# Three streams for two in a transformer of two layers: first attention, experts with cross attention, and last layer of three successive sequences

## The reference

```python
# block 0: self attention (causal) and cross attention to ctx, 16 heads of 8, one projection
y = softmax(mask(q @ k.T / sqrt(8))) @ v + softmax(qc @ kc.T / sqrt(8)) @ vc
x = x + y @ Wp + bp                                 # x normed before q, k, v, qc
# block 0: all 8 experts (128 -> 512 -> 128), weighted by a softmax over the top 2 logits
x = x + sum_e w[:, e] * (relu(xn @ W1[e] + b1[e]) @ W2[e] + b2[e])
# block 1: one-head attention to ctx (256 x 256 scores)
x = x + softmax(q1 @ k1.T) @ v1
# block 1: 16 heads of 64; values mixed per token and head from the top 2 of 8 expert values,
# outputs gathered per token over the top 2 of 8 output experts
v[h] = sum_e mix[t, h, e] * (xn @ Wv[e]);  at[h] = softmax(q[h] @ k[h].T / 8) @ v[h]
x = x + sum_h sum_e mask_o[t, h, e] * (at[h] @ Wo[e])
```

## Time and profile before

| | us |
|---|---|
| median of 3 runs | 1716.87 (1716.63 to 1721.53) |
| profiled execution, its own time | 1711.72 |
| its span, first to last instruction | 1710.0 |
| TensorE busy | 1310.1 |
| VectorE busy | 718.0 |
| ScalarE busy | 488.1 |
| mean granted clock of TensorE | 0.718 |

### The profile page before, as it was taken

The page is one execution under the profiler, slowest core; times in us unless marked ns, Lnnn a source line. Parts: engine busy times, 40 slices in busy tenths (PEclk is TensorE's granted clock), DMA queues, the critical chain, the costliest instruction groups (busy, mean ns, idle before and its releaser), DMA issues.

```text
span 1710.0 us, 21323 instructions
## 1 busy us (share of the span) xinstructions
PE 1310.1 (77%) x8530; PEld 1008.1 (59%) x8530; DVE 718.0 (42%) x1958; ACT 488.1 (29%) x1003; POOL 77.1 (5%) x134
## 2 busy tenths in 40 slices
PE   2777668887679777896788777897688876897566
PEld 2446545775458654685457654596457754586366
DVE  2623492335822385225813376214832349122700
ACT  0233314224133232333143232333132231332120
POOL 0010001000010000100010000100010000100000
PEclk9657766787667875697658875697666976677655
DMA  5000010311012110301103110301103101121131
GB/s 157 7 1 4 0 31 4 64 44 26 12 28 43 38 28 10 64 19 28 34 1 64 44 29 10 58 13 41 25 10 64 44 16 22 26 41 38 37 59 46
DMA packets 197498, 56.85 MB, mean 33 GB/s; under 512 B 173029, under 2 KB 193303, under 8 KB 197399
## 3 DMA queue, kind: packets, MB, share of 16 engines
q1 hardware_dynamic: 195318, 51.30, 14.2%
q10 hardware_dynamic: 2080, 4.19, 0.8%
HBM read 31.36 MB, written 24.12 MB: 32 GB/s over the span
## 4 chain that ended last, share of the span: by engine, by line
PE 60%; DVE 23%; ACT 7%; issue 4%; DMA 3%; SPq 0%; ACTq 0%; DVEq 0%
PE bank L942 8%; PE bank L766 8%; PE bank L792 7%; DVE negmax L1179 6%; PE bank L692 6%; PE bank L904 4%; PE bank L618 4%; ACT pa L1012 3%; DVE negc L1331 3%; PE bank L925 3%; PE bank L707 2%; DVE qk_lo L1323 2%; DMA at<-at_d 2%; PE bank L956 2%; PE bank L717 2%
## 5 line engine op out<-in xcount | busy, mean ns | idle before, releaser
L1012 ACT ACTIVATE pa<-bank 128x512 f32<-128x512 f32 x224 | 123.4, 597 | 351.5 <-PE bank L707 266.2
L942 PE MATMUL bank<-vb,pb 128*128 128x65 f32 x1024 | 147.2, 315 | 12.2 <-issue 12.2
L942 PEld LDWEIGHTS bank<-vb,pb 128*128 128x128 f32 x1024 | 145.8, 232 | 16.4 <-issue 16.3
L766 PE MATMUL bank<-xnT_a,w 128*128 128x256 f32 x512 | 145.9, 436 | 0.0
L1179 DVE TENSOR_REDUCE negmax<-bank 128x2 f32<-128x512 f32 (+1 forms) x224 | 138.8, 682 | 16.2 <-PE bank L653 11.6
L1029 ACT ACTIVATE pa<-bank,b_c 128x256 f32<-128x256 f32 x256 | 107.3, 470 | 127.8 <-PE bank L766 126.4
L792 PEld LDWEIGHTS bank<-w,pa 128*128 128x128 f32 x1024 | 124.1, 193 | 3.0
L792 PE MATMUL bank<-w,pa 128*128 128x128 f32 x1024 | 124.1, 276 | 0.0
L766 PEld LDWEIGHTS bank<-xnT_a,w 128*128 128x128 f32 x512 | 106.7, 219 | 21.9 <-issue 7.0
L1087 ACT ACTIVATE pb<-bank 128x512 f32<-128x512 f32 x128 | 69.5, 595 | 169.7 <-PE bank L908 169.4
L692 PE MATMUL bank<-pa,va 128*32 128x256 f32 (+1 forms) x1024 | 101.8, 550 | 16.4 <-ACT pa L1012 15.9
(11 more groups left out here) (231 smaller groups left out, 1972.3 us busy)
## 6 DMA issues: line engine op xcount, KB each, us to landing
v_d<-vb SPq DMA_DIRECT2D x16, 512.0 KB, 5.1
vb<-v_d SPq DMA_DIRECT2D x16, 512.0 KB, 5.7
at_d<-at SPq DMA_DIRECT2D x32, 256.0 KB, 2.1
at<-at_d SPq DMA_DIRECT2D x32, 256.0 KB, 4.3
pv_d<-pvs SPq DMA_DIRECT2D x8, 512.0 KB, 2.8
pvs<-pv_d SPq DMA_DIRECT2D x16, 256.0 KB, 4.3
w<-in_L_ffn_W_dram ACTq DMA_DIRECT2D x1, 2048.0 KB, 10.4
bd<-mix_d SPq DMA_DIRECT2D x128, 8.0 KB
```

The lines of the kernel that those rows point to most:

```text
L766: mm = pe.matmul(BA[u % 2][:, c * T:(c + 1) * T], w1[:, e, f:f + P], xnT_a[:, :], start=True, stop=True)
L942: mm = pe.matmul(BB[2 + qt][:, i * (DH + 1):(i + 1) * (DH + 1)], pb[:, h % NPB, kt * T + qt * P:kt * T + (qt + 1) * P], vb[:, kt, h, :], s ...
L1012: nc.scalar.activation(pa[:, e % NPA, :], BA[e % 2][:, :], ACT.Exp, scale=SC0).then_inc(S["a_ex"], 1)
```

## The change

The two streams become three. A keeps the first attention and the next sequence's input norm; X takes a_norm2, the router, the experts (step a_expert is divided in a_hid, one hidden half, and a_yout, one expert's output) and the cross attention; B stays. X starts 1.03 and B 2.06 periods after A, so that three successive sequences are at work. HOLD is a new table. The banks are dealt out anew: three for A, two for X, three for B. a_max goes in groups of three tiles, b_split and b_max over three banks; the values of the first attention, the mixed values and the two halves of b_attend have one bank each where they had two, X's hidden tiles one, X's outputs one. So steps gain waits for the copy out of a bank that they had not: values(n) waits for output n-1, the second half of b_mix and of b_attend for the first, the fourth turning in a_shift and a_heads for the first tile's use.

x_f has two halves by the sequence's parity, and takes the place of x_a up to the first expert's accumulation; cxT_a has two; the input norm gets its own xn and xnT_f; the experts' hidden tiles and the cross attention's operands move from pa to a new hx of three tiles; pa has 8 tiles, pb 6. f_load stands before a_heads, and its load of x_f waits for the first accumulation of two sequences back. The number of matmuls, activations and VectorE instructions is as before.

```diff
-        BA, BB = banks[:4], banks[4:]
+        BA, BX, BB = banks[:3], banks[3:5], banks[5:]
...
-        x_f = sb("x_f", [P, NT, C])
+        x_f = sb("x_f", [P, 2, NT, C])
         cx_f = sb("cx_f", [P, NT, CC])
         x_a = sb("x_a", [P, NT, C])
         xnT_a = sb("xnT_a", [P, T])
-        cxT_a = sb("cxT_a", [CC, T])
+        cxT_a = sb("cxT_a", [CC, 2, T])
+        xnT_f = sb("xnT_f", [P, T])
...
-        NPA = 9
+        NPA = 8
...
-        hT = pa[:, 0:4, :].rearrange("p u (c n) -> p u c n", c=2)
+        hx = sb("hx", [P, 3, 512])
+        hT = hx[:, :, :].rearrange("p u (c n) -> p u c n", c=2)
...
-        NPB = 8
+        NPB = 6
...
-        ln["f"]["xn"] = ln["a"]["xn"]
-        y = ln["a"]["xn"]
-        xn_a, xn_b = ln["a"]["xn"], ln["b"]["xn"]
+                      xn=sb(f"xn_{s}", [P, NT, C])) for s in "abf"}
+        y = ln["f"]["xn"]
+        xn_a, xn_b, xn_f = ln["a"]["xn"], ln["b"]["xn"], ln["f"]["xn"]
...
-        NBLK = NS // 4
+        NBLK = (NS + 2) // 3
...
-        OUT_AT = {4: 0, 5: 1, 7: 2, 8: 3, 11: 4, 12: 5}
+        OUT_AT = {4: (0, 1), 7: (2,), 8: (3,), 11: (4, 5)}
...
-        RUNS = {"a_max": 2, "a_score": 7, "a_expert": 4, "b_score": 2}
-        LAG = 0.04
         HOLD = {
-            "a_stack": 1.0, "a_values": 1.29, "a_max": (3.44, 7.52, 2.92, 10.2), "a_shift": 3,
-            "a_score": (1.92, 2.01), "a_lastpv": 2.07, "a_heads": 4.0, "a_project": 1.88, "a_norm2": 4.26,
-            "a_norm2_apply": 1.04, "a_router": 6.19, "a_expert": (4, 4.01), "a_b2": 12, "c_norm": 3.31,
-            "f_norm": 0.77, "f_load": 0, "c_norm_apply": 1.29, "c_qkv": 3.77, "f_norm_apply": 1, "c_max": 1.57, "c_turn": 1.62,
-            "c_out": 1.74, "b_norm": 2.87, "b_norm_apply": 3, "b_gates": 2.98, "b_split": 0.98, "b_top2": 3,
-            "b_max": 1.4, "b_shift": 7.07, "b_score": (4, 4, 4, 4), "b_mix": 4.5,
-            "b_attend": 4, "b_weigh": 5, "b_gather": 5, "b_out": 6}
-
-        def share(step):
-            name, i = step
-            return HOLD[name][i // RUNS[name]] if name in RUNS else HOLD[name]
-
+            "a_stack": 2, "a_values": 3, "a_max": 3, "a_shift": 5, "a_score": 4, "a_lastpv": 4, "f_load": 0, "a_heads": 5,
+            "a_project": 5, "f_norm": 8, "f_norm_apply": 3,
+            "a_norm2": 8, "a_norm2_apply": 2, "a_router": 4, "a_hid": 3, "a_yout": 6, "a_b2": 4, "c_norm": 8,
+            "c_norm_apply": 2, "c_qkv": 5, "c_max": 4, "c_turn": 4, "c_out": 4,
+            "b_norm": 9, "b_norm_apply": 2, "b_gates": 5, "b_split": 2, "b_top2": 0, "b_max": 2.2, "b_shift": 4,
+            "b_score": 4, "b_mix": 5, "b_attend": 6, "b_weigh": 7, "b_gather": 3, "b_out": 5}
 
         STEPS_A = [("a_stack", u) for u in range(8)] + [("a_values", 0)]
         STEPS_A += [("a_max", m) for m in range(NBLK)] + [("a_shift", 0)]
-        STEPS_A += [("a_score", n) for n in range(2 * PER_J)] + [("a_lastpv", 0), ("a_heads", 0), ("a_project", 0)]
-        STEPS_A += [("f_load", 0), ("a_norm2", 0), ("a_norm2_apply", 0), ("a_router", 0)]
-        STEPS_A += [("a_expert", e) for e in range(E)] + [("a_b2", 0)]
-        STEPS_A += [("c_norm", 0), ("f_norm", 0), ("c_norm_apply", 0), ("c_qkv", 0), ("f_norm_apply", 0),
-                    ("c_max", 0), ("c_turn", 0), ("c_out", 0)]
+        STEPS_A += [("a_score", n) for n in range(2 * PER_J)] + [("a_lastpv", 0), ("f_load", 0), ("a_heads", 0), ("a_project", 0)]
+        STEPS_A += [("f_norm", 0), ("f_norm_apply", 0)]
+        STEPS_X = [("a_norm2", 0), ("a_norm2_apply", 0), ("a_hid", 0), ("a_router", 0), ("a_hid", 1)]
+        for e in range(E):
+            STEPS_X += [("a_hid", 2 * e + 2)] if e + 1 < E else []
+            STEPS_X += [("a_yout", e)]
+            STEPS_X += [("a_hid", 2 * e + 3)] if e + 1 < E else []
+        STEPS_X += [("a_b2", 0), ("c_norm", 0), ("c_norm_apply", 0), ("c_qkv", 0), ("c_max", 0), ("c_turn", 0), ("c_out", 0)]
         STEPS_B = [("b_norm", 0), ("b_norm_apply", 0), ("b_gates", 0)]
         STEPS_B += [("b_split", u) for u in range(4)] + [("b_top2", 0)] + [("b_split", u) for u in range(4, 8)] + [("b_top2", 1)]
         STEPS_B += [("b_max", 0), ("b_max", 1), ("b_top2", 2)] + [("b_max", m) for m in range(2, 8)] + [("b_shift", 0)]
-        STEPS_B += [("b_score", 0), ("b_score", 1), ("b_mix", 0), ("b_mix", 1)] + [("b_score", p) for p in range(2, 4)]
-        for hg in range(1, 4):
-            STEPS_B += [("b_attend", hg - 1), ("b_score", 2 * hg + 2), ("b_score", 2 * hg + 3)] if hg < 3 else [("b_attend", 2)]
-        STEPS_B += [("b_attend", 3), ("b_weigh", 0), ("b_gather", 0), ("b_gather", 1), ("b_out", 0)]
-
-        def merged(lag):
+        STEPS_B += [("b_score", 0), ("b_score", 1), ("b_mix", 0), ("b_mix", 1), ("b_score", 2), ("b_attend", 0)]
+        STEPS_B += [("b_score", 3), ("b_score", 4), ("b_attend", 1), ("b_score", 5), ("b_score", 6), ("b_attend", 2)]
+        STEPS_B += [("b_score", 7), ("b_attend", 3), ("b_weigh", 0), ("b_gather", 0), ("b_gather", 1), ("b_out", 0)]
+
+        def merged():
 
             timed = []
...
-            for steps, offset in ((STEPS_A, 0.0), (STEPS_B, 1.0 + lag)):
-                total, at_ = sum(share(step) for step in steps), 0
+            for steps, offset in ((STEPS_A, 0.0), (STEPS_X, 1.03), (STEPS_B, 2.06)):
+                total, at_ = sum(HOLD[name] for name, _ in steps), 0
...
-                        if q > 0:
-                            sp.wait_ge(S["a_x1"], upto("a_x1", 0))
-                        sp.dma_start(x_f[:, :, :], x_tiles[:, q * NT:(q + 1) * NT, :]).then_inc(S["f_in"], 16)
+                        if q > 1:
+                            sp.wait_ge(S["a_acc"], upto("a_acc", 1 - 2 * E))
+                        sp.dma_start(x_f[:, q % 2, :, :], x_tiles[:, q * NT:(q + 1) * NT, :]).then_inc(S["f_in"], 16)
...
-                        sc, qt, _, gp = MAXS[4 * m]
+                        tiles = range(3 * m, min(3 * m + 3, NS))
...
+                        for c in range(4):
+                            for n in tiles:
+                                sc, qt, j, gp = MAXS[n]
+                                rows = slice(32 * j, 32 * j + 32)
                                 if m > 0 and c == 0:
...
-                        bank, pair, i = BA[2 + n % 2], j // 2, j % 2
+                        bank, pair, i = BA[2], j // 2, j % 2
                         pe.wait_ge(S["a_ex"], upto("a_ex", 2 * PER_J * pair + (8 if sc == CROSS else 2 * PER_J)))
                         if sc == SELF:
                             pe.wait_ge(S["a_sl"], upto("a_sl", 6 * pair + 6))
-                        if n >= 2:
-                            pe.wait_ge(S["a_ot"], upto("a_ot", n - 1))
+                        if n >= 1:
+                            pe.wait_ge(S["a_ot"], upto("a_ot", n))
...
-                    def hidden(u):
+                    def a_hid(u):
                         e, fp = u // 2, u % 2
-                        if u >= 2:
-                            pe.wait_ge(S["a_ha"], upto("a_ha", u - 1))
+                        if u == 0:
+                            pe.wait_ge(S["a_xc"], upto("a_xc", 1))
+                            pe.wait_ge(s_experts, 32)
+                        else:
+                            pe.wait_ge(S["a_ha"], upto("a_ha", u))
                         for c in range(2):
                             f = (2 * fp + c) * P
-                            mm = pe.matmul(BA[u % 2][:, c * T:(c + 1) * T], w1[:, e, f:f + P], xnT_a[:, :],
+                            mm = pe.matmul(BX[0][:, c * T:(c + 1) * T], w1[:, e, f:f + P], xnT_a[:, :],
                                            start=True, stop=True)
                         mm.then_inc(S["a_h"], 1)
...
+                    def a_yout(e):
                         pe.wait_ge(S["a_ha"], upto("a_ha", 2 * e + 2))
-                        if e == 1:
+                        if e == 0:
                             pe.wait_ge(S["a_lgc"], upto("a_lgc", 1))
-                        if e >= 2:
-                            pe.wait_ge(S["a_acc"], upto("a_acc", e - 1))
+                        else:
+                            pe.wait_ge(S["a_acc"], upto("a_acc", e))
                         for t in range(NT):
                             for f in range(FC):
-                                mm = pe.matmul(BA[2 + e % 2][:, t * P:(t + 1) * P],
-                                               hT[:, (2 * e + f // 2) % 4, f % 2, t * P:(t + 1) * P], w2[:, e, f, :],
+                                mm = pe.matmul(BX[1][:, t * P:(t + 1) * P],
+                                               hT[:, (2 * e + f // 2) % 3, f % 2, t * P:(t + 1) * P], w2[:, e, f, :],
...
-                        else:
-                            pe.wait_ge(S["b_ve"], upto("b_ve", NT))
-                        for i in range(T8):
-                            g = T8 * half + i
-                            for t in range(NT):
-                                rows = slice(64 * t, 64 * t + 64)
```

(17 more changed lines are left out.)

278 lines of the change are left out of this document (128 added, 150 removed).

## The result

The changed kernel takes 1835.72 us (median of 4 runs, 1833.88 to 1841.98); the kernel before took 1719.06 beside it. The ratio is 1.0685, 95% interval 1.0652 to 1.0718: slower by 117 us, where 1685 us had been forecast in a range up to 1790.

The account below looks back on a forecast made before the run. TensorE was taken to set most of the time, VectorE one stretch of each period. Period 75 + 83 + 9 + 9.7 + 5 + 3.5 = 185 us; 572 + 6 x 185 = 1682, given as 1685 us; range 1555 to 1790.

Parts of the forecast that it names:

- The ends: Set-up and the stretches at the run's start and end without three full streams: 572 us in all, give or take 15.
- DVE's stretch: Part of each period set by VectorE (row maxima, splits, top-2): 63.5 us of work, taken as 75 us at 85% busy.
- PE's work: TensorE's matmuls in the period's other stretches: 100 us at today's clocks, 17 saved by a higher clock, 83 remain.
- Waits inside PE's steps: New single-bank waits in values, b_mix, b_attend and a_heads that no other stream can fill: 9.7 us a period.
- 5 for b_attend 0: Wait before b_attend's first step for the mixed values' round trip, partly covered by other steps: 5 us a period.
- b_mix's lost side-by-side run: b_mix's two halves run one after the other instead of alternating: 3.5 us a period, bounds 0 to 5.
- X's single banks at nothing: Stream X's one-bank chain, 33 us, runs under A and B within eight tenths of a period, so costed at nothing.
- Rival 2: Single-bank pauses in TensorE's steps keep its clock low; period 200 us, time 1772 us; chance 0.30.
- Its sign: Rival 2's mark in the new profile: successive sequences' marks 190 us or more apart, clock at 0.72 or under.
- Rival 3: Experts' 48 us at clock 1.00 run at 0.50 between narrow matmuls; period about 221, time 1900 us; chance 0.06.
- theory T: Expectation from the follow-up experiments, not the prediction: the third stream itself spreads the dense work, whatever the banks.

Follow-up runs that it names:

- the filler: Two-stream kernel with b_attend on one bank (1788.34 us), plus two fp32 matmuls with unread results put in place of the wait: 1764.50 us.
- 1696: Three-stream kernel with b_attend in half-steps on one bank and b_mix's two halves side by side on two banks: 1695.86 us.
- 1704: Kernel 1696 with the values as steps of their own and the mixed values (vb) loaded back ahead of bd: 1704.22 us.
- 1707: Three-stream kernel with two banks for b_attend and b_mix, values as own steps, vb loaded earlier, b_attend in half-steps, no pause step: 1706.78 us.
- two banks alone: Three-stream kernel with b_attend's second half on a second bank borrowed from the scores, other one-bank forms kept: 1786.30 us.
- the pause alone: Three-stream kernel with an empty step of 8 shares (about 11 us) in stream B's plan before b_attend 0: 1795.11 us.

## Why the prediction was wrong

By its own steps:

- *The ends*, 572 us: measured 580. The first attention alone ends at 145.2 for 147, the first x_mid stands at 274 for 272, the last layer alone within 3 us; the 8 us are in X of the last sequence beside B (160 for 152). Right within the 15 that were given.
- *DVE's stretch*, 75 us: measured 82. DVE's work in it was sized right (62.6 for 63.5 us), its density was not, 76% for the assumed 85%. 7 us of the error a period. And the stretch was taken as given by the order's shares; shifting B shows it was a choice of the offset, worth 39, 52 and 61 us in three kernels.
- *PE's work*, "64.2 us at 0.62 to 0.85, 17 us saved, 83 remain": this is the step that failed. Measured, in place of 83 + 3.5, are 109.2 us; 23 of the 24 us by which the period was missed (DVE's 7 more are nearly offset by 6 less of waiting). The work at full clock was about right (77 us for 87 - 11.4). But the granted clock over PE's stretches went from 0.76 to 0.70, where 17 us had been booked for a rise. The bounds of the term were too narrow in kind: "nothing saved" kept the experts' stretch at 1.00, as if only the narrow stretches had a clock to gain or lose. What took its place: where b_attend stood in the dense stretch at 1.00, its single bank and the wait for the round trip now put pauses, and b_attend and its neighbours run at the lower level. That such pauses do it is shown in two streams and argued in three (one bank for b_attend in two streams: 41 us of longer matmuls beside 31 of waiting; the filler took 24 us off by adding work; the cut into half-steps took 100 us of busy time off with no idle time saved).
- *Waits inside PE's steps*, 9.7 us a period, and 5 for b_attend 0: idle time in PE's stretches was 17.8 in all for 23.7. One by one: between b_attend's halves 0.73 for 1.0; before b_attend 0 4.0 in this period and 5.1 in the mean of the six, for 5; b_mix 11.5/8 = 1.4 for 1.8; the values (23.6 - 16.4)/8 = 0.9 for 2.55, the one that was well off (there are three waits for the copy a sequence, as forecast, but of 0.65 us, and the waits for the exponentials fell from 15.9 to 7.1 us in all). As idle time they were priced well, and as a cause of a lower clock at nothing.
- *b_mix's lost side-by-side run*, 3.5 us: the same change in two streams cost 34/8 = 4.3, and L925 5.6 a sequence; the changed kernel's line has (81.6 - 48.8)/8 = 4.1 more. Near the upper bound of 5.
- *X's single banks at nothing*: 21.9 us before L765, 2.7 a sequence, not nothing; but the same form costs the two-stream kernel 60 us of idle time and 107 in all, so that most of it was covered, as argued.

Rival 2, "the period does not shrink", had the mechanism: pauses of about 1 us from single banks keep the clock down. Its sign, marks 190 or more apart at a clock of 0.72 or under, is what came (209 and 0.717). It was given 0.30 and a period of 200 us; its price was short too, since it let the clock only stay at 0.62 in the outer stretches, and the level fell inside, so that the time lies above the whole range. The argument held against it, that 9.7 us of new pauses are less than what a third stream covers, compared microseconds of idle time, where the place of a pause counted. Rival 3, that the experts lose their clock, came true in part: their two groups took 65 us more.

The Trainium skill, "TensorE: Matmul & The Clock Gate", section "A second HAM failure mode: psum-queue depth-cycling", says that brief idle between groups of matmuls, from cycling through PSUM banks, makes the clock go down and up again. The kernel with one bank for b_attend and the one with its pauses filled (1788 and 1764 us, share 0.42 and 0.65) agree in this: filling the pause returned the level. Here the idle time comes from one bank used twice in a row, and not from going through several. The rule would have made rival 2 the likeliest, and the direction bears it out; it gives no price.

What stays open: why b_attend's share in half-steps falls from 0.64 (1696) to 0.47 (1704 and 1707) once the values are steps of their own and vb is loaded earlier, though idle time falls; it isn't the second bank. Open too is why shortening the waits before b_attend by 41 us left the time unchanged, and how the single bank and the long wait share the low level of b_attend in the changed kernel: two banks alone brought the share from 0.27 to 0.38, the pause alone to 0.55, and two banks with the values' steps and a wait of 9.5 us left it at 0.26. Drawing the experts together into b_attend's stretch would test theory T by itself. One such order was written, but in it the engines wait for one another in a circle, so it has no time, and T by itself stays untested. Shown is only that the third stream is no obstacle to a clock of 0.77; without the shift of B it brings a period of 190 us for 197.

## What to carry to other kernels

Before a stream is added, write down for each PE step that loses a bank which engine it then waits for in its middle, and cut the step there, so that the other streams' steps fill the wait; a wait inside a dense stretch is to be priced at its length and again at the slower matmuls around it (31 and 41 us here). Put the stretches that another engine bounds (here the row maxima of two streams) at different places of the period: one offset was worth 2 to 3% here. And look at busy time, not at the mean clock or the idle time alone: the mean was 0.717 and 0.718 in two kernels 117 us apart.

## What the runs showed of the hardware

- Adding 128 matmuls (49.6 us of them) in pauses of 0.7 to 0.8 us made a kernel 24 us faster: the pauses' 24 us went, and all other matmuls together ran 51 us shorter (b_attend's share at the high level 0.65 for 0.42).
- One and the same step stands at either level in one execution: in the two-stream kernel b_attend 0 takes 3.76 us for 32 matmuls at 720 us, and at 1110 us 20 of them take 4.50. An edit elsewhere (one bank for the values) moved b_attend's busy time from 147 to 130 us. Judged by these 17 us, an estimate: some 15 us of difference between two such kernels can come from this alone.
- Matmuls on rows 0 to 63 and on 64 to 127, issued in turns, run side by side. In the two-stream kernel the same 512 take 48.8 us in turns and 93.2 one half after the other, at unlike shares of the high level. With all of them at the low level they take 58.9 us in the kernel with one bank for the values (in turns, two banks) and twice that in the one with all one-bank forms (one half after the other, one bank):

```profile
L925 PE MATMUL bank<-pvs,bd 64*128 64x64 f32 x512 | 117.3, 420 | 11.5 <-ACT vb L1092 11.5
```
